# A reordered turn: x transposes before the last gate/up group, LayerNorm scale on the centred heads, second values before the last down products

## The reference, cut to what matters

```python
x = x + tanh(g_xattn) * mlstm(q=layernorm(x), k=ctx, v=ctx)   # 8 x 512 rows, 16 heads of 64
#   per head: h = (C / normalizer) @ v ; hn = (h - mean) * rsqrt(var + eps)
#   hn = hn * ln_scale            (per column, 1024 values)
x = x + tanh(g_ffn) * ffn(layernorm(x))
#   router logits -> top 2 of 16 experts, each silu(x@gate) * (x@up) @ down, width 512
#   plus a shared expert, silu(x@sg) * (x@su) @ sd, width 1024
```

## Time and profile before

| | |
|---|---|
| median of 3 runs | 2911.98 us (2910.44 to 2918.33) |
| profiled execution, own time | 2916.85 us |
| its span, first to last instruction | 2915.3 us |
| stretch of `mix_block`, roughly | 0 to 1120 us of the span |
| PE busy over the span | 2775.5 us, 95% |
| DVE busy over the span | 1868.2 us, 64% |
| ACT / POOL busy over the span | 35% / 34% |
| mean granted PE clock | 0.985 of full speed |

### The profile page before, as it was taken

How to read it: one execution, slowest core, us unless ns; L and a number is a source line. 1 busy time by engine, 2 the same in 40 slices (tenths; PEclk the granted TensorE clock), 3 DMA queues, 4 the chain that set the end, 5 groups by cost and what they waited for, 6 DMA issues and landing times.

```text
span 2915.3 us, 49270 instructions
## 1 busy us (share of the span) xinstructions
PE 2775.5 (95%) x17322; PEld 2283.1 (78%) x17323; DVE 1868.2 (64%) x2800; ACT 1016.4 (35%) x1948; POOL 996.1 (34%) x1148
## 2 busy tenths in 40 slices
PE   3899999999999996999999999999999999999999
PEld 2777777777777775888888888888888888888887
DVE  4888888888888864554455545545455457767676
ACT  4544444444444432233234423423333331111111
POOL 2343434343443433344344334334334311111111
PEclk7899999999999998999999999999999999999999
DMA  7445545455545543244444344344434326666665
GB/s 223 150 146 163 164 151 156 147 174 160 160 146 160 168 160 130 87 146 149 151 147 148 144 153 149 144 151 151 151 144 149 121 102 201 194 195 189 199 184 180
DMA packets 243471, 458.24 MB, mean 157 GB/s; under 512 B 99697, under 2 KB 131825, under 8 KB 240625
## 3 DMA queue, kind: packets, MB, share of 16 engines
q1 hardware_dynamic: 116976, 333.62, 34.2%
q0 software_dynamic: 34880, 73.10, 8.1%
q10 hardware_dynamic: 91488, 49.82, 6.3%
HBM read 358.96 MB, written 115.31 MB: 163 GB/s over the span
## 4 chain that ended last, share of the span: by engine, by line
PE 60%; DVE 0%; issue 0%; ACT 0%; DVEq 0%
PE p_g_b L1585 20%; PE p_up_b L1585 20%; PE p_y_b L1571 19%; PE p_h_b L1558 1%; DVE x_t_b L1450 0%; DVE th_b L1462 0%; DVE x L1492 0%; DVE x L1483 0%; ACT th_b L1399 0%; DVE y_b L1494 0%; DVE x L1479 0%; DVE h_b L1467 0%; DVE xt_lo_b L1456 0%; DVE stage L1492 0%; DVE ht_lo_b L1439 0%
## 5 line engine op out<-in xcount | busy, mean ns | idle before, releaser
L1277 POOL DMA_INDIRECT xn<-mid_xn,idx_q x284 | 303.6, 1069 | 513.1 <-DVE x_t_b L1450 425.0
L1585 PE MATMUL p_g_b<-w_hi,xt_hi_b 128*128 128x512 f32 x840 | 334.6, 398 | 18.9 <-DVE xt_lo_b L1456 16.1
L1571 PE MATMUL p_y_b<-w_hi,ht_hi_b 128*128 128x512 f32 x840 | 327.5, 390 | 1.9 <-DVE ht_lo_b L1439 1.9
L1585 PE MATMUL p_g_b<-w_lo,xt_hi_b 128*128 128x512 f32 x840 | 328.8, 391 | 0.0
L1585 PE MATMUL p_g_b<-w_hi,xt_lo_b 128*128 128x512 f32 x840 | 328.4, 391 | 0.0
L1585 PE MATMUL p_up_b<-w_hi,xt_lo_b 128*128 128x512 f32 x840 | 328.2, 391 | 0.0
L1585 PE MATMUL p_up_b<-w_lo,xt_hi_b 128*128 128x512 f32 x840 | 327.9, 390 | 0.0
L1585 PE MATMUL p_up_b<-w_hi,xt_hi_b 128*128 128x512 f32 x840 | 327.8, 390 | 0.0
L1571 PE MATMUL p_y_b<-w_lo,ht_hi_b 128*128 128x512 f32 x840 | 327.5, 390 | 0.0
L1571 PE MATMUL p_y_b<-w_hi,ht_lo_b 128*128 128x512 f32 x840 | 327.3, 390 | 0.0
L1439 DVE TENSOR_TENSOR ht_lo_b<-p_h_b,ht_hi_b 128x512 fp32r<-128x512 f32 x74 | 51.0, 689 | 367.5 <-ACT ht_hi_b L1354 367.5
(11 more groups left out here) (220 smaller groups left out, 5595.0 us busy)
## 6 DMA issues: line engine op xcount, KB each, us to landing
mid_y<-y_b SPq DMA_DIRECT2D x73, 512.0 KB, 2.6
stage<-mid_g_row SPq DMA_DIRECT2D x64, 512.0 KB, 5.0
stage<-in_eg SPq DMA_DIRECT2D x16, 2048.0 KB, 8.4
stage<-in_eu SPq DMA_DIRECT2D x16, 2048.0 KB, 14.7
stage<-in_ed SPq DMA_DIRECT2D x16, 2048.0 KB, 18.8
mid_y<-in_x SPq DMA_DIRECT2D x34, 512.0 KB
stage<-in_x SPq DMA_DIRECT2D x32, 512.0 KB
stage<-in_ctx_t ACTq DMA_DIRECT2D x32, 512.0 KB, 8.8
```

The costliest lines, as they stand in the source:

```text
L1277: nc.gpsimd.indirect_dma_start(out=xg_parts[:, n, :], out_offset=None, in_=xn_flat, in_offset=bass.IndirectOffsetOnAxis(ap=idx_q[:, n:n + ...
L1571: last = nc.tensor.matmul(p_y[n][:, :], a[:, k, :], b[:, GUP + k, w], start=(k == 0 and m == 0), stop=(k == FE // P - 1 and m == 2))
L1585: mm = nc.tensor.matmul(out[:, :], a[:, k, :], w[:, k, o:o + FE], start=(k == 0 and m == 0), stop=(k == KD - 1 and m == 2))
```

## The change

It rewrites `TURN` and the offset of D, splits D1's POOL part off as M1, and splits the semaphore of the last gate/up group.

- PE's order becomes A2 B0 H1 A3 B2 Y1 B1 Y2 Y3 B3 Y4 A5 N1 B4 G1 N2 A6 E3 G2 G3 G4 G5 Q2 G6 E4 K7 Q3 K8.
- ACT's becomes A3 B2 A1 B3 A5 N1 N2 T1 A9 F2 E3 C1 Q2 Q3 U1, DVE's A2 B0 H1 A3 D1 E1 B1 A4 E2 J1 N1 L1 N2 A6 S1 Q1 B5 E3 C1 F3 C2 E4 U1 (DVE's old B4 is now B5). On SP F1 stands before E2, and D1's fill is issued one turn number later, behind X1 as before.
- M1 on POOL multiplies the centred heads in `uc` by `lns` once ACT has squared them, ahead of C2's power. D1 on DVE then writes the scaled result at once, and E1 follows without POOL between them. D1 runs in the next turn.
- In K8 the three gate matmuls come first and signal `g_ps`, then the three up matmuls signal `gu_ps`. ACT's tanh waits for `g_ps`, DVE's second product for `gu_ps`.

```diff
-        TURN = ("A2", "B0", "V1", "H1", "A3", "B2", "O1", "W1", "Y1", "E1", "P1", "A4", "E2", "A1", "B1", "W2", "Y2",
-                "F1", "Y3", "A5", "J1", "Y4", "N1", "W3", "B3", "A6", "L1", "N2", "T1", "W4", "S1", "Q1", "G1", "W5",
-                "A9", "F2", "B4", "A7", "A8", "E3", "G2", "R1", "G3", "C1", "F3", "G4", "X1", "G5", "Q2", "C2", "G6",
-                "E4", "W6", "Z1", "U1", "D1", "K7", "K8", "Q3")
+        TURN = ("A2", "B0", "V1", "H1", "A3", "D1", "B2", "O1", "W1", "Y1", "E1", "P1", "A1", "B1", "W2", "Y2",
+                "Y3", "A4", "F1", "E2", "W3", "B3", "Y4", "A5", "J1", "N1", "L1", "B4", "G1", "N2", "T1", "W4", "A6", "S1", "Q1",
+                "B5", "W5", "A9", "F2", "A7", "A8", "E3", "G2", "R1", "G3", "C1", "F3", "G4", "X1", "G5", "Q2", "M1", "C2",
+                "G6", "E4", "W6", "Z1", "K7", "Q3", "K8", "U1")
...
-                  "D": 0, "E": -1, "N": -1, "G": -1, "P": 0, "K": -1, "U": -1, "H": -2, "Y": -2, "J": -2,
+                  "D": -1, "M": 0, "E": -1, "N": -1, "G": -1, "P": 0, "K": -1, "U": -1, "H": -2, "Y": -2, "J": -2,
...
-            def stage_d(part, b, j):
-                c = b * CPB + j
-                if part == 1:
-                    if isinstance(c, int) and c == 0:
-                        pool.wait_ge(act_set, 4)
-                    ge(pool, o_rdy, c + 1)
-                    nc.gpsimd.tensor_tensor(sq_flat, sq_flat, lns[:, :], ALU.mult).then_inc(scaled_rdy, 1)
+            def stage_m(part, b, j):
+                c = b * CPB + j
+                u = uc[:, j % 2, :, 0:DH]
+                if c == 0:
+                    pool.wait_ge(act_set, 4)
+                pool.wait_ge(sq_rdy, 2 * c + 2)
+                nc.gpsimd.tensor_tensor(u, u, lns[:, :].rearrange("p (h d) -> p h d", h=NH), ALU.mult
+                                        ).then_inc(scaled_rdy, 1)
...
-                act.wait_ge(gu_ps, c + 1)
+                act.wait_ge(g_ps, c + 1)
...
-                if part == 4 and j < CPB - 1:
+                if part == 5 and j < CPB - 1:
...
+                    dve.wait_ge(scaled_rdy, c + 1)
                     dve.wait_ge(hrs_rdy, c + 1)
...
-                    dve.wait_ge(scaled_rdy, c + 1)
+                    dve.wait_ge(o_rdy, c + 1)
...
+                dve.wait_ge(gu_ps, c + 1)
                 nc.vector.scalar_tensor_tensor(out=th[:, :], in0=th[:, :], scalar=0.5, in1=p_up[:, :],
                                                op0=ALU.mult, op1=ALU.mult).then_inc(h_rdy, 1)
...
-                if k == KD - 1:
-                    last.then_inc(gu_ps, 1)
+                else:
+                    for out, o, done in ((p_g, 0, g_ps), (p_up, FE, gu_ps)):
+                        for m, (a, w) in products:
+                            last = nc.tensor.matmul(out[:, :], xt[:, a, k, :], w[:, k, o:o + FE], start=False, stop=(m == 2))
+                        last.then_inc(done, 1)
```

More of the change, by code:

```diff
@@ L179, in mix_block @@
         h_ps, hh_sb, hl_sb = sem("h_ps"), sem("hh_sb"), sem("hl_sb")
-        gu_ps, tanh_rdy, silu_rdy, h_rdy = sem("gu_ps"), sem("tanh_rdy"), sem("silu_rdy"), sem("h_rdy")
+        g_ps, gu_ps, tanh_rdy, silu_rdy, h_rdy = sem("g_ps"), sem("gu_ps"), sem("tanh_rdy"), sem("silu_rdy"), sem("h_rdy")
         y_ps, z_rdy = sem("y_ps"), sem("z_rdy")
@@ L474, in stage_e @@
                             in_=tok_all[:, c:c + 1], in_offset=None).then_inc(done, 16)
-            schedule({"L": stage_l, "A": stage_a, "C": stage_c, "D": stage_d, "E": stage_e})
+            schedule({"L": stage_l, "A": stage_a, "C": stage_c, "M": stage_m, "E": stage_e})
             ge_apart(pool, past, (scat0, 16 * NCH), (scat1, 16 * NCH))
@@ L980, in gate_up @@
                     pe.wait_ge(xl_sb, 2 * c + k // 4 + 1)
[L981 to L984, removed]
-                if k == KD - 1:
-                    last.then_inc(gu_ps, 1)
+                products = tuple(enumerate(((0, w_hi), (1, w_hi), (0, w_lo))))
+                if k < KD - 1:
+                    for m, (a, w) in products:
+                        for out, o in ((p_g, 0), (p_up, FE)):
+                            nc.tensor.matmul(out[:, :], xt[:, a, k, :], w[:, k, o:o + FE],
+                                             start=(k == 0 and m == 0), stop=False)
+                else:
+                    for out, o, done in ((p_g, 0, g_ps), (p_up, FE, gu_ps)):
+                        for m, (a, w) in products:
+                            last = nc.tensor.matmul(out[:, :], xt[:, a, k, :], w[:, k, o:o + FE], start=False, stop=(m == 2))
+                        last.then_inc(done, 1)
             def stage_y(part, b, j):
```

## The result

The changed kernel takes **3063.9 us** (median of 5 runs, 3055.8 to 3066.7) against 2913.7 for the one before (2910.4 to 2918.3). The ratio is 1.051 (95% interval 1.050 to 1.0525): slower, by 150 us. The forecast was 2992, at most 3055. So the sign was right, and the waits came as forecast; the loss of 150 us is nearly twice the 80 us forecast, because the falls of the clock cost several times what was set down for them. The profiled execution after took 3055.8 us, the fastest of its five, so the two traces stand 3055.8 - 2916.9 = 139 us apart.

The account below looks back on a forecast made before the run. PE was taken as the bound, busy 94 us of 100. Waits of 61 us and clock falls of 19 took the profiled 2916.85 us to 2997, so the median to 2992 us; range 2945 to 3055.

Parts of the forecast that it names:

- Q3 ahead of K8, 1.05 us gained: At the turn's end, six gate/up matmuls cover ACT's copy of Q3 before A2: 1.05 us a turn gained.
- M1, D1 and K8's split at 0: POOL's product moved off the path to E1, and the tanh half a group earlier: each worth 0.
- A5's 0.59: PE's wait for DVE's `rows` before A5 goes entirely: 0.59 us a turn gained, bounds 0 and 0.59.
- G1's wait, 1.82: New PE wait at G1 for `xt`, behind ACT's table load and N1's copy: mean 1.82 us a turn, lower bound 0.5.
- E3's wait, 1.8: New PE wait at E3 for N2's copies, the second half of `xt`: 1.8 us a turn, bounds 1.6 and 2.3.
- The sum of the waits: Waits added at G1 and E3 less those gained at A2 and A5: 1.98 us a turn, 61 us in all.
- The clock, 0.6 a turn: PE's clock falls after the new waits: 16 falls of 1.2 us, 19 us in all, bounds 0 and 74.
- Rival 4: PE's clock falls twice in nearly every turn, 62 x 1.2 = 74 us: 3047 us, chance 0.12.
- The port, rival 3: M1 on POOL holds DVE's line 775, so H1 waits about 1.3 us: up to 31 us more, 3023, chance 0.1.

Follow-up runs that it names:

- run 1: The changed kernel with the old middle of the turn, new head and tail kept: 2882.6 us, ratio 0.989 to the kernel before.
- run 3: The kernel before with the new middle of the turn alone, Q3, D1 and last gate/up group as before: 3096.6 us, ratio 1.061.
- run 7: The kernel before with Q3 ahead of K8, the last group split and U1 behind K8, nothing else: 2914.0 us, ratio 0.998.
- run 8: The kernel before with M1, the later D1 and K8's split, Q3 and U1 left where they were: 2900.3 us, ratio 0.994.
- run 4: The changed kernel with A5 ahead of Y4 instead of behind it: 3040.2 us, ratio 1.042 to the kernel before.
- run 5: The changed kernel with N2 ahead of B4 and G1: 3008.4 us, ratio 1.033 to the kernel before.
- run 2: The changed kernel with 12 unread matmuls a turn, six ahead of G1's wait and six behind N2: 3003.9 us, ratio 1.031.
- run 6: The changed kernel with six unread matmuls a turn behind N2 only: 3019.6 us, ratio 1.035 to the kernel before.
- run 10: The changed kernel with the old middle of the turn, and M1 behind POOL's power (C2): 2876.9 us, ratio 0.988.
- run 9: The changed kernel with the old middle of the turn, and A6 behind G1 instead of ahead of N2: 2925.1 us, ratio 1.003.

## Why the prediction was right or wrong

- **Q3 ahead of K8, 1.05 us gained:** right for the change as a whole. The wait before A2 is gone, and the head and tail together bring 33 us with the old middle (run 1) and with the new (run 3), 1.05 x 31. By itself it would have been worth 3 us (run 7). The forecast had set M1, D1 and K8's split at 0, and that was wrong: without Q3 they bring 16 us (run 8), and without M1 and D1 Q3 brings next to nothing. That the sum was right is in part luck.
- **A5's 0.59:** right in the profile, no such wait in the steady turns.
- **G1's wait, 1.82:** measured 1.8. The chain is the one named: with A5 a step earlier it halves (run 4).
- **E3's wait, 1.8:** 1.6 without an A6, 1.9 + 0.35 with one, so 1.9 on average. That it is N2's copies was shown by run 5. The small excess lies in the turns with an A6, where I credited the kernel before with a wait of 0.6 at A6, while it had 4.3 us in 900, 0.3 for each such turn. The sum of the waits was forecast as 1.98 a turn and measured as 2.0, 63 us instead of 61: this part was right.
- **The clock, 0.6 a turn:** this is the step that failed. I took 1.2 us for a fall and a fall in half of the turns, 19 us. Measured, the turn has 4.2 - 2.0 = 2.2 us that no wait explains, and filling the idle time gives 60 us back (run 2). Over the whole execution the granted clock was 0.961 in 3054.2 us after and 0.985 in 2915.3 before, so that 119 - 44 = 75 us more were lost to it; this is an upper estimate, since PE also idles in some of these stretches. Waits of 63 and a clock of 75 make 138 of the 139 us. Both factors of the term were half of the truth. In windows of 1 us laid end to end from 150 to 1100 us, the clock leaves 1.00 in 26 separate stretches, about one a turn; the kernel before has 2. And the 26 are 4.9 us long on average, which at half clock loses 2.4 us each. The one in the turn shown lasts from about 511.7 to 518.5 us. The price could have been read beforehand, because the fall of the earlier trace rows is longer than the 2 us that I took. Its neighbouring windows in the kernel before are

```profile
446.00:448.00 2.00, 0.41 (x4) 0.40 (x4) 1.93 (x7) 0.00 (x0) 0.22 (x1) 0.89 0.90 184
450.00:452.00 2.00, 2.00 (x27) 1.53 (x27) 0.78 (x2) 0.44 (x1) 0.00 (x0) 0.76 0.02 4
```

  With 0.50 between them that is (0.11 + 0.50 + 0.24) x 2 = 1.7 us lost, not 1.2. Rival 4, which had 0.12, comes near with its 62 x 1.2 = 74 us, but by luck: it has two short falls in nearly every turn, and what happened is one fall of twice the price. What sets how often the clock falls stays open (runs 4 and 6).
- **The start:** the first tanh comes at 116.3 us instead of 108.7, 7.6 us that the forecast did not have. PE's waits there moved to the values behind the decay products. It wasn't taken apart further.
- **The port, rival 3:** in the change M1 (2.20 us) held DVE's line 776 for 1.02 us instead of 0.17, until M1's own end, while the reduction in front kept its 1.22 us, and `absf` took 0.28 us throughout. The Trainium skill, "SBUF — State Buffer", section "Who interferes with whom", says that a DVE instruction with two SBUF inputs contends with a GpSimd one that reads SBUF, and that a reduction doesn't. The trace agrees. Its price was nil here, as H1 never waited in the steady turns, and a few us at most in run 10.
- **The range:** it reached 3055, 9 us short. Its upper end, 3047 for the clock's worst case and 8 us more, left little room for a slower start beside a clock term that came out at that worst case.

## What to carry to other kernels

When a dependent step is moved, count what stands between it and its user afterwards on the waiting engine, and what now stands in front of its copies on the copying engine; here the first gave 1.6 to 1.9 us of wait and the second about 1 (run 4). On PE the added waits cost some 2.1 times their length (4.2 us for 2.0), since the clock falls behind them. This factor is no constant: 0.7 us of waits taken away gave back 0.7 (run 4), and 0.5 us added cost 1.4 (43 us, run 9). So take the clock's share from the repeated pattern, and not from a single fall. And test the parts of a merged change apart: this one hid a gain of 33 us under a loss of 181.

## What was unexpected of the hardware

Matmuls whose results nobody reads made a kernel 60 us faster (run 2), by keeping the granted clock at 0.98 instead of 0.94. Waits of 1.4 us at most, one or two a turn, were enough to lower the mean granted clock from 0.99 to 0.97 (run 9), while the 0.8 us before A2 in nearly every turn of the kernel before left it at 1.00 from 500 to 600 us.
